# Four row buffers in the scoring stages, and 32 x 32 turns on VectorE in the first layer's chunk softmax, in a graph-attention kernel

## The chip, the cores and the metric

One core of a Trainium2 chip. The metric is the device time of one launch in microseconds (us); the kernel before took 2799.43 us (median of 3 runs, 2797.33 to 2800.22). A change of about 0.2% (5.6 us) is what a measurement of this kernel can tell from none.

## What is computed

Three graph attentions over 3125 nodes with 256 features and 50000 edges sorted by destination, with residual sums and two layer norms. The first attention has 8 heads, the second one, the third 4 (with a vector for each of 64 edge types). Cut to the first:

```python
feat = (h @ fc_w.T).reshape(n, heads, out_feats)
el = jnp.sum(feat * attn_l, axis=-1); er = jnp.sum(feat * attn_r, axis=-1)
e = jax.nn.leaky_relu(el[src] + er[dst], 0.2)
m = jax.ops.segment_max(e, dst, num_segments=n)
ex = jnp.exp(e - m[dst])
ssum = jax.ops.segment_sum(ex, dst, num_segments=n)
rst = jax.ops.segment_sum(feat[src] * (ex / ssum[dst])[..., None], dst, num_segments=n)
```

## The kernel before

**Tiles and stages.** The edges are cut into 416 items of 128 edges, one edge in each partition, none of which crosses a block of 128 destinations. Eight items are a group (52 groups), 32 items a turn or chunk (13). The program is a row of stages, and at each stage's start every engine but GpSimd (POOL) waits for the others: items, node1, score1, sum1, node2, score2, soft2, sum2, node3, score3, soft3, sum3, final. The engines meet through semaphores that are written out by hand; each runs its own instruction list in order.

**Gathers (lines 700 to 752).** POOL issues one indirect DMA for each item and each table (line 735): 416 of layer 1's features (`tab_feat1`, 256 features and 8 `el` terms), 416 of layer 2's, 416 rows of K and 416 of V. The rows land in a ring of 8 slots of 8 items (4 slots for K). A slot is gathered anew when its reader has released it: in sum1 by `slot_used` on the multiply of line 1961, in sum2 by `sum_mm` from the matmuls of line 929. POOL runs ahead of the stages as far as the ring lets it.

**Scores.** For each group, SyncE broadcasts the block-local destinations of its 1024 edges to all partitions, 128 KB (lines 574 and 547; in score2 and score3 a second DMA brings the low source numbers or the types). VectorE compares them with its partition number and so has one-hot rows (line 1761 in score1, 1531 in score2; in score3 ScalarE does it, line 1275). TensorE multiplies them with the tables of `er` and `el` (line 971; lines 849 and 852), VectorE reads the products (1767; 1568 and 1577, between them the one-hot 1554 of the next group) and then makes the one-hots of the group after the next. There are two buffers of broadcast rows (`bcast`), of one-hots (`onehot_t`) and of products, used in turn (s % 2). SyncE issues a group's rows when `onehot_made[s % 2]` shows that the one-hots of two groups before are made. Once in two groups TensorE loads 16 block numbers into registers (`blocks`, line 822), since the matmuls address their table by them.

**sum1 (lines 983 to 1062 and 1836 to 2001).** The first layer's softmax is done chunk by chunk beside its weighted sums. For a chunk `c + 1`, VectorE adds `el` and `er` when the last of its four slots has landed (`make_logits`); TensorE turns the logits so that two items of a head lie in each of 128 lanes (`transposed`); VectorE scans them for running maxima in both directions (`lane_tops`); TensorE turns the two columns of lane ends into one row of partition 0 (`lane_ends`, lines 995 and 996), where VectorE scans over the lanes (`stitch`); TensorE turns the two rows of carries back into columns (`carries`, 1001 and 1002), and VectorE scans again with them and computes the exponentials (`numerators`). TensorE turns the result back (`shares`, line 1009) and makes the factors (`factors`, 1014) by which the open bank of sums is rescaled (`rescale`). Between these steps stand the four groups of the chunk in work: `build(c, half, g)` makes the one-hot rows (1954) and weighted rows (1961, 1965) of group g in two buffers used in turn, and TensorE adds them up in PSUM (line 1024, 16 instructions for a group). VectorE's order in a period is

```python
rescale(c); make_logits(c + 1); build(1); lane_tops(c + 1); build(2)
stitch(c + 1); build(3); numerators(c + 1); factor_terms(c + 1); build(c + 1, 0)
```

Of the kernel before, what the change touches and what calls it, by code (L numbers as in the profile page):

```python
# [29 lines left out]
P = 128  # L30
# [67 lines left out]
def graph_layers(nc, a, out):  # L98
    ctx = ExitStack()
    with ctx:  # L100
# [88 lines left out]
        def views(*sizes):  # L189
            got, at = [], 0  # L190
            for n in sizes:
# [36 lines left out]
        bcast = v[0][:, 0:GROUP * P].bitcast(U8).rearrange("p (s a e) -> p s a e", s=2, a=2)  # L228
        bcast_words = v[0][:, 0:GROUP * P].bitcast(I16).rearrange("p (s a e) -> p s a e", s=2, a=2)
# [17 lines left out]
        gate0, gate1, from_left, from_right, before_row, after_row = (v[7][0:1, k * P:(k + 1) * P] for k in range(6))  # L247
        tail_row = v[7][0:1, 6 * P:6 * P + H1 * (LANES + 1)].rearrange("p (h j) -> p h j", h=H1)
        crossing, factor_rhs, factor, carry_cols = v[8], v[9], v[10], v[11]
# [71 lines left out]
        bcast_in = [sem(f"item_rows_broadcast{s}") for s in range(2)]  # L321
# [13 lines left out]
        logits_made, logits_t, ends_made, ends_t, stitched, carried, numer_made, shares_in, factor_in, factor_made = (  # L335
            sem("chunk_" + k) for k in ("logits_made", "logits_transposed", "lane_ends_made", "lane_ends_in_rows",
                                        "carries_made", "carries_in_columns", "numerators_made", "shares_in_psum",
# [79 lines left out]
        TR_BANK, W_BANK, ROW_BANK = 0, 1, 2  # L417

        def broadcasts(layer):

            return 16 * HALF + 32 * HALF * (layer - 1) if layer else 0

        @block.sync
        def _(sp):
# [108 lines left out]
            def score_rows(layer, name, first):  # L533
# [35 lines left out]
            with nc.sync.Fori(0, TURNS) as u:  # L569
                for s in range(SLOTS):  # L570
# [3 lines left out]
                    sp.dma_start(bcast_words[:, s % 2, 1], row.partition_broadcast(P)).then_inc(bcast_in[s % 2], 16)  # L574
# [62 lines left out]
        def _(pool):  # L637
# [13 lines left out]
            for credit in slot_used + onehot_made + score_read + sort_row_used:  # L651
# [102 lines left out]
        def _(pe):  # L754
# [76 lines left out]
            def gat_scores(layer, name, heads):  # L831
# [5 lines left out]
                with nc.tensor.Fori(0, TURNS) as u:  # L837
                    for s in range(SLOTS):
# [3 lines left out]
                        pe.wait_ge(onehot_made[s % 2], nth(u, s) + (layer * HALF + 2))  # L842
# [17 lines left out]
            def pair_scores(layer, name):  # L860
# [3 lines left out]
                with nc.tensor.Fori(0, TURNS) as u:  # L864
                    for s in range(SLOTS):
# [3 lines left out]
                        pe.wait_ge(onehot_made[s % 2], nth(u, s) + (layer * HALF + 2))  # L869
# [87 lines left out]
            def er_pass(name):  # L957
# [4 lines left out]
                with nc.tensor.Fori(0, TURNS) as u:  # L962
                    for s in range(SLOTS):
# [3 lines left out]
                        pe.wait_ge(onehot_made[s % 2], nth(u, s) + 2)  # L967
# [15 lines left out]
            def chunk_sums(name):  # L983
# [9 lines left out]
                def lane_ends(c):  # L993
                    pe.wait_ge(ends_made, c + 1)
                    nc.tensor.matmul(ps[0:1, ROW_BANK, 0:P], heads_top[:, 0:1], ident[:], start=True, stop=True)
                    nc.tensor.matmul(ps[0:1, ROW_BANK, P:2 * P], tops[:, SPAN - 1:SPAN], ident[:], start=True,
                                     stop=True).then_inc(ends_t, 1)

                def carries(c):
                    pe.wait_ge(stitched, c + 1)  # L1000
                    nc.tensor.matmul(ps[:, ROW_BANK, 2 * P:2 * P + 1], before_row, ones[0:1, 0:1], start=True, stop=True)
                    nc.tensor.matmul(ps[:, ROW_BANK, 2 * P + 1:2 * P + 2], after_row, ones[0:1, 0:1], start=True,
                                     stop=True).then_inc(carried, 1)

                def shares(c):
                    pe.wait_ge(numer_made, c + 1)
                    by_lane = ps[:, W_BANK, 0:SPAN].rearrange("p (j x h) -> p x h j", x=2, h=H1)
# [1218 lines left out]
```

## Time and profile before

| | before |
|---|---|
| median of 3 runs | 2799.43 us |
| the profiled execution's own time | 2800.09 us |
| its span in the trace | 2798.3 us |
| TensorE's mean granted clock | 0.75 of full speed |
| busy: PE, PEld, DVE, ACT, POOL | 61%, 44%, 54%, 15%, 59% |

The span is what the trace covers; 1.8 us lie around it. PE is TensorE's matmuls, PEld its weight loads, DVE is VectorE, ACT ScalarE, POOL GpSimd, SP SyncE. "q" behind an engine's name is its sequencer. A row of a timeline has the start, the duration, the engine, the line of the kernel, the operation, what it writes and reads, and in brackets how long the engine had been idle and what ended that idle time ("issue": nothing that the profile shows). No engine is near 100%, so that a reader has to go by stages. On the time axis the stages lie about so: score1 143 to 265 us, sum1 to 786, node2 to 884, score2 to 1027, soft2 to 1048, sum2 to 1503, node3 to 1627, score3 to 2150, soft3 and sum3 to 2690, final to 2798.

### The profile page before, as it was taken

To read this page: it belongs to the slowest core of one execution; us is meant where nothing else is said; L and a number is where in the kernel's file an instruction comes from. 1 tells how busy PE (TensorE), PEld (TensorE's weight loads), DVE (VectorE), ACT (ScalarE), POOL (GpSimd) and SP (SyncE) were. 2 spreads that over 40 slices of the span, in tenths; PEclk is the share of its full clock that TensorE was granted. 3 is DMA by queue.
4 is the path that set the end of the run, shared out by engine and by line. 5 is a ranking of instruction groups with operands and counts; after the bars stand their busy time and mean duration, and the time that the engine had idled before them with its cause. 6 is when DMAs were issued, how large, how long until landed. Compare 5 with 4: busy or idle time off the path is not lost.

```text
span 2798.3 us, 30721 instructions
## 1 busy us (share of the span) xinstructions
PE 1710.9 (61%) x7623; PEld 1226.0 (44%) x7624; DVE 1518.8 (54%) x2334; ACT 430.0 (15%) x909; POOL 1659.1 (59%) x1791
## 2 busy tenths in 40 slices
PE   3844555555587437655655977777776465565654
PEld 1433434343455436444443445555554344444443
DVE  3245766756745876333334646666766633333348
ACT  0200000000021000000001444444442100000024
POOL 0072777777302816777773057777777777777720
PEclk8855777777788558687776977778878667768679
DMA  0363333333213633333332344444444333333322
GB/s 25 104 154 89 97 105 106 105 106 106 56 54 106 172 93 95 104 104 105 105 104 64 107 122 130 131 130 131 131 130 120 98 105 104 105 105 104 105 64 69
DMA packets 166454, 290.04 MB, mean 104 GB/s; under 512 B 37842, under 2 KB 113035, under 8 KB 166411
## 3 DMA queue, kind: packets, MB, share of 16 engines
q0 software_dynamic: 79872, 219.91, 27.4%
q1 hardware_dynamic: 86539, 69.66, 9.4%
q8 instruction: 14, 0.23, 0.0%
q14 instruction: 29, 0.24, 0.0%
HBM read 272.74 MB, written 16.68 MB: 103 GB/s over the span
## 4 chain that ended last, share of the span: by engine, by line
POOL 46%; issue 22%; DVE 11%; PE 9%; DMA 9%; SPq 1%; POOLq 1%; DVEq 1%; ACT 0%; ACTq 0%
POOL row_space L735 45%; DMA arena<-rows_block_dst 6%; PE ps L1024 2%; DVE arena L1961 2%; PE ps L810 2%; PE ps L1075 2%; DVE arena L1531 1%; DMA row_space<-tab_k,index_slot 1%; DMA row_space<-tab_feat,index_slot 1%; DVE arena L1954 1%; PE ps L1077 1%; DVE arena L1761 1%; POOL index_slot L710 1%; PE ps L802 1%; PE ps L775 1%
## 5 line engine op out<-in xcount | busy, mean ns | idle before, releaser
L735 POOL DMA_INDIRECT row_space<-tab_feat,index_slot x832 | 832.6, 1001 | 368.7 <-issue 235.0
L929 PE MATMUL ps<-row_space,arena 128*128 128x257 f32 (+1 forms) x1664 | 581.8, 526 | 383.0 <-DVE row_space L1722 383.0
L929 PEld LDWEIGHTS ps<-row_space,arena 128*128 128x128 f32 x1664 | 445.5, 274 | 519.2 <-issue 419.4
L1721 DVE TENSOR_TENSOR row_space<-row_space,ps 128x2048 f32<-128x2048 f32 x104 | 237.6, 2285 | 579.6 <-DMA row_space<-tab_v,index_slot 303.4
L735 POOL DMA_INDIRECT row_space<-tab_v,index_slot x416 | 402.8, 968 | 123.8 <-issue 118.8
L735 POOL DMA_INDIRECT row_space<-tab_k,index_slot x416 | 394.0, 947 | 123.8 <-issue 116.4
L1024 PE MATMUL ps<-arena 128*128 128x265 f32 x832 | 253.4, 469 | 102.6 <-DVE arena L1965 53.0
L883 PE MATMUL ps<-row_space,arena 128*128 x832 | 288.9, 508 | 0.0
L710 POOL COPY index_slot<-src_i 128x16 int32 (+1 forms) x104 | 25.3, 243 | 405.1 <-SPq L426 404.8
L1024 PEld LDWEIGHTS ps<-arena 128*128 128x128 f32 x832 | 190.8, 235 | 154.5 <-issue 112.4
L1217 ACT COPY acc<-ps 128x265 f32<-128x265 f32 (+2 forms) x75 | 28.3, 377 | 1420.6 <-PE ps L929 919.4
L883 PEld LDWEIGHTS ps<-row_space,arena 128*128 128x128 f32 x832 | 198.6, 250 | 39.0
L1613 DVE TENSOR_TENSOR arena<-row_space,ps 128x1024 f32<-128x1024 f32 x104 | 126.4, 1215 | 162.7 <-DMA row_space<-tab_k,index_slot 131.2
L877 PE MATMUL ps<-rel_stack,arena 128*128 128x64 bf16 x416 | 88.3, 212 | 125.8 <-DVE arena L1621 111.7
L1715 DVE TENSOR_TENSOR arena<-ps,block_dst 128x1024 f32<-128x1024 f32 x104 | 126.1, 1213 | 14.3 <-ACT ps L1203 14.3
L1621 DVE TENSOR_TENSOR arena<-arena,ps 128x1024 f32<-128x1024 f32 x104 | 127.0, 1221 | 9.7 <-DVE arena L1613 5.4
L877 PEld LDWEIGHTS ps<-rel_stack,arena 128*128 128x128 bf16 x416 | 41.1, 99 | 186.7 <-DVE arena L1621 158.1
L1603 DVE TENSOR_REDUCE scores<-arena 128x2048 f32 (+1 forms) x52 | 118.5, 2280 | 0.0
L1961 DVE TENSOR_TENSOR arena<-row_space,ps 128x2048 f32<-128x2048 f32 x52 | 118.4, 2276 | 0.0
L849 PE MATMUL ps<-el_parts,arena 128*128 128x25 bf16 x1248 | 60.8, 183 | 81.5 <-DVE arena L1531 75.3
L1275 ACT ACTIVATE arena<-arena,minus_type_no 128x1024 bf16<-128x1024 uint8 x52 | 59.7, 1147 | 285.3 <-PE ps L883 277.0
L971 PE MATMUL ps<-er_parts,arena 128*128 x416 | 56.2, 199 | 72.5 <-DVE arena L1761 60.0
(316 smaller groups left out, 2091.6 us busy)
## 6 DMA issues: line engine op xcount, KB each, us to landing
arena<-rows_block_dst SPq DMA_DIRECT2D x156, 128.0 KB
row_space<-tab_feat,index_slot POOLq DMA_INDIRECT x832
arena<-rows_src_low SPq DMA_DIRECT2D x52, 128.0 KB
arena<-rows_type SPq DMA_DIRECT2D x52, 128.0 KB
row_space<-tab_k,index_slot POOLq DMA_INDIRECT x416
row_space<-tab_v,index_slot POOLq DMA_INDIRECT x416
arena<-in_x_t SPq DMA_DIRECT2D x50, 128.0 KB, 2.2
tab_feat<-arena SPq DMA_DIRECT2D x25, 132.0 KB, 1.8
```

The lines of the kernel that those rows point to most:

```text
L735: nc.gpsimd.indirect_dma_start(wide_rows[:, s, g, 0:(D if n else WIDE)], None, table, bass.IndirectOffsetOnAxis(ap=index_slot[:, s, g:g + ...
L849: nc.tensor.matmul(ps[:, bank, at:at + w], onehot_t[:, s % 2, 0, e], el_parts[:, k, 0:w], start=k == 0, stop=k == 2)
L877: nc.tensor.matmul(relation, type_onehot[:, s % 2, e], rel_stack[:, 0, :], start=True, stop=False)
L883: last = nc.tensor.matmul(ps[:, bank, at:at + D], query_onehot[:, s % 2, g * P:(g + 1) * P], query[:, bass.ds(bs[g], 1), :].rearrange("p a ...
L929: last = nc.tensor.matmul(ps[:, SUM_BANKS:2 * SUM_BANKS][:, bank, 0:width].rearrange("p a d -> p (a d)"), onehots_of[:, s, g, :], wide_row ...
L1024: last = nc.tensor.matmul(ps[:, SUM_BANKS:2 * SUM_BANKS][:, bass.ds(banks[s % 2 * GROUP + g], 1), 0:AW].rearrange("p a d -> p (a d)"), one ...
L1603: vec.tensor_reduce(by_item(H3)[:, bass.ds(u * STEP + s * GROUP, GROUP), :], pair_product[:, s % 2].rearrange("p i (h d) -> p i h d", h=H3 ...
L1613: then(vec.tensor_tensor(pair_product[:, z, items, :].rearrange("p i (h d) -> p i h d", h=H3), rows[:, s, items, :].rearrange("p i (h d) - ...
L1621: vec.tensor_tensor(pair_product[:, z, items, :], pair_product[:, z, items, :], ps[:, 2 * half:2 * half + 2, :].rearrange("p q (i d) -> p ...
L1715: vec.tensor_tensor(onehots_of[:, s], ps[:, SHARE_BANK:SHARE_BANK + 1, IOTA_AT:IOTA_AT + P].broadcast_to([P, GROUP, P]), block_dst[:, bass ...
L1721: vec.tensor_tensor(row, row, share.unsqueeze(3).broadcast_to([P, GROUP, heads, D // heads]), ALU.mult)
L1961: vec.tensor_tensor(weighted[:, z, :, 0:D].rearrange("p i (h d) -> p i h d", h=H1), wide_rows[:, half * SLOTS + g, :, 0:D].rearrange("p i ...
```

## The change

First, `bcast` has four buffers of rows, one for each group of a turn, with four semaphores; the one-hots still have two. SyncE gets its credit for them once more (two for each of the two semaphores), and the waits of TensorE on `onehot_made` are one higher, so that only SyncE runs two groups further ahead. This is in score1, score2 and score3.

Second, in sum1 the lane ends and the carries are turned by VectorE, in 32 x 32 blocks: eight `vec.transpose` for the two columns of ends and eight for the two rows of carries; the four small matmuls and their three waits are gone. The softmax of chunk `c + 1` is no longer spread between the groups: `lane_tops`, `stitch`, `numerators` and `factor_terms` run in one piece behind `build(2)` and ahead of `build(3)`. TensorE turns the shares and makes the factors ahead of the fourth group. The shares have two banks of PSUM, used in turn; the factors move to the bank of the turned logits. TensorE's loop holds two chunks instead of one.

```diff
-        bcast = v[0][:, 0:GROUP * P].bitcast(U8).rearrange("p (s a e) -> p s a e", s=2, a=2)
+        bcast = v[0].bitcast(U8).rearrange("p (s a e) -> p s a e", s=SLOTS, a=2)
...
-            for credit in slot_used + onehot_made + score_read + sort_row_used:
+            for credit in slot_used + onehot_made + onehot_made + score_read + sort_row_used:
...
-                            sp.dma_start(bcast_words[:, s % 2, k], row.partition_broadcast(P)).then_inc(bcast_in[s % 2], 16)
+                            sp.dma_start(bcast_words[:, s, k], row.partition_broadcast(P)).then_inc(bcast_in[s], 16)
...
-                        pe.wait_ge(onehot_made[s % 2], nth(u, s) + (layer * HALF + 2))
+                        pe.wait_ge(onehot_made[s % 2], nth(u, s) + (layer * HALF + 3))
...
-                    if not last:
-                        lane_ends(c + 1)
                     banks, cleared = sum_banks(c, 2)
                     group_sums(c, 2, banks, cleared)
                     if not last:
-                        carries(c + 1)
+                        shares(c + 1, 1 - half)
+                        factors(c + 1)
                     group_sums(c, 3, banks, cleared)
-                    if not last:
-                        shares(c + 1)
-                        factors(c + 1)
...
-                dve.wait_ge(bcast_in[z], nth(u, s) * 32 + (32 + broadcasts(layer)))
-                vec.tensor_scalar(onehot_t[:, z], bcast[:, z], part_no[:], None,
+                dve.wait_ge(bcast_in[s], u * 32 + (32 + broadcasts(layer)))
+                vec.tensor_scalar(onehot_t[:, z], bcast[:, s], part_no[:], None,
                                   ALU.is_equal).then_inc(onehot_made[z], 1)
...
+                    all_but(0)
+                    for k, edge in enumerate((heads_top[:, 0:32], tops[:, SPAN - 32:SPAN][:, ::-1])):
+                        for q in range(0, P, 32):
+                            last = vec.transpose(end_rows[:, k * P + q:k * P + q + 32], edge[q:q + 32])
+                    then(last)
...
+                    for k in range(2):
+                        for q in range(0, P, 32):
+                            turned = vec.transpose(carry_blocks[q:q + 32, k * 32:(k + 1) * 32],
+                                                   row_block[:, (4 + k) * P + q:(4 + k) * P + q + 32])
+                    then(turned)
...
-                    each(vec.tensor_copy(carry_cols[:, 0:2], ps[:, ROW_BANK, 2 * P:2 * P + 2]))
...
                     build(c, half, 1)
-                    if not last:
-                        lane_tops(c + 1)
                     build(c, half, 2)
                     if not last:
-                        stitch(c + 1)
+                        soft_chunk(c + 1)
+                        factor_terms(c + 1)
                     build(c, half, 3)
                     if not last:
-                        numerators(c + 1)
-                        factor_terms(c + 1)
                         build(c + 1, 1 - half, 0)
```

## Rows read from the trace of the kernel before

**Rows 1.** The page's chain that ended last: shares of the span.
```profile
POOL row_space L735 45%; DMA arena<-rows_block_dst 6%; PE ps L1024 2%; DVE arena L1961 2%; PE ps L810 2%; PE ps L1075 2%; DVE arena L1531 1%; DMA row_space<-tab_k,index_slot 1%; DMA row_space<-tab_feat,index_slot 1%; DVE arena L1954 1%; PE ps L1077 1%; DVE arena L1761 1%; POOL index_slot L710 1%; PE ps L802 1%; PE ps L775 1%
```

**Rows 2.** Stretch of score2: length, busy us (count) of each engine, PE clock, DMA share, GB/s.
```profile
884.00:1027.00 143.00, 62.77 (x1665) 58.64 (x1666) 116.32 (x216) 0.00 (x0) 91.41 (x68) 0.50 0.55 154
```

**Rows 3.** Line 735's own view: ns min/median/max, releasers of its engine's idle time.
```profile
L735 POOL DMA_INDIRECT row_space<-tab_k,index_slot x416: 942/946/975, 1627.2 to 2148.4; - x139
...
  PE ps L929: 63.3, 1
  DVE arena L1961: 61.3, 18
```

**Rows 4.** Timeline of POOL, sum1: start us, us, instruction, idle before and releaser.
```profile
284.56 1.06 POOL L735 DMA_INDIRECT row_space<-tab_feat,index_slot  x1 [56.09 <-DVE arena L1961]
...
520.73 0.97 POOL L735 DMA_INDIRECT row_space<-tab_feat,index_slot  x1 [0.16 <-POOL index_slot L710]
...
734.22 0.95 POOL L735 DMA_INDIRECT row_space<-tab_feat,index_slot  x1 [0.30 <-issue]
```

**Rows 5.** Line 1531's own view, score2's one-hots on VectorE.
```profile
L1531 DVE TENSOR_SCALAR arena<-arena,part_no x52: 1277/1286/1521, 887.4 to 1022.5; 128x2048 bf16<-128x2048 uint8 x52
```

**Rows 6.** Timeline of score2, all engines.
```profile
1002.87 1.28 DVE L1531 TENSOR_SCALAR arena<-arena,part_no 128x2048 bf16<-128x2048 uint8 x1 [0.79 <-DMA arena<-rows_block_dst]
...
1004.74 0.39 SPq L547 DMA_DIRECT2D arena<-rows_block_dst  x1
...
1004.98 1.28 DVE L1531 TENSOR_SCALAR arena<-arena,part_no 128x2048 bf16<-128x2048 uint8 x1
```

**Rows 7.** The chain in order of time: start us, us, what.
```profile
951.04 3.87 DMA arena<-rows_block_dst
...
1004.74 3.01 DMA arena<-rows_block_dst
```

**Rows 8.** Timeline of TensorE, score2.
```profile
1002.02 0.23 PE L849 MATMUL ps<-el_parts,arena 128*128 128x25 bf16 x3 [1.72 <-DVE arena L1531]
...
1004.21 0.26 PE L849 MATMUL ps<-el_parts,arena 128*128 128x25 bf16 x3 [0.99 <-DVE arena L1531]
...
1007.43 0.26 PE L849 MATMUL ps<-el_parts,arena 128*128 128x25 bf16 x3 [2.03 <-issue]
```

**Rows 9.** Line 822's own view, PE's register load.
```profile
L822 PEldq TENSOR_LOAD <-block_i x78: 1102/1105/1298, 138.5 to 2131.2; - x78
```

**Rows 10.** Timeline of TensorE, score1, with gathers running and after they stopped.
```profile
190.63 2.18 PE L971 MATMUL ps<-er_parts,arena 128*128 x16 [2.17 <-DVE arena L1761]
194.58 2.19 PE L971 MATMUL ps<-er_parts,arena 128*128 x16 [1.76 <-DVE arena L1761]
...
240.41 2.21 PE L971 MATMUL ps<-er_parts,arena 128*128 x16 [2.12 <-issue]
```

**Rows 11.** Timeline of VectorE, start of sum1.
```profile
270.07 0.28 DVE L1876 COPY arena<-ps 1x128 f32<-1x128 f32 x1 [1.10 <-PE ps L996]
...
272.49 0.16 DVE L1904 COPY arena<-ps 128x2 f32<-128x2 f32 x1 [0.71 <-PE ps L1002]
```

**Rows 12.** Timeline of VectorE, one period of sum1.
```profile
491.52 0.59 DVE L1859 TENSOR_TENSOR arena<-row_space,scores 128x256 f32<-128x256 f32 x1 [11.81 <-DMA row_space<-tab_feat,index_slot]
...
495.96 0.67 DVE L1867 TENSOR_TENSOR_SCAN arena<-arena,ps 128x256 f32<-128x256 bf16 x1
...
502.14 0.28 DVE L1876 COPY arena<-ps 1x128 f32<-1x128 f32 x1 [1.34 <-PE ps L996]
...
503.66 0.16 DVE L1890 TENSOR_TENSOR arena<-arena 1x8 f32<-1x8 f32 x1
...
515.85 1.22 DVE L1954 TENSOR_TENSOR arena<-ps,block_dst 128x1024 f32<-128x1024 f32 x1
517.00 2.28 DVE L1961 TENSOR_TENSOR arena<-row_space,ps 128x2048 f32<-128x2048 f32 x1
```

**Rows 13.** Groups by line: busy us, mean ns, idle before.
```profile
L1928 DVE TENSOR_SCALAR arena<-iota_free,arena 128x128 f32<-128x128 f32 x12 | 3.4, 280 | 0.0
```

More of the change, by code:

```diff
@@ L320, in graph_layers @@
         slot_used = [sem(f"rows_used{s}") for s in range(2 * SLOTS)]
-        bcast_in = [sem(f"item_rows_broadcast{s}") for s in range(2)]
+        bcast_in = [sem(f"item_rows_broadcast{s}") for s in range(SLOTS)]
         onehot_made = [sem(f"onehot_made{s}") for s in range(2)]
@@ L416, in graph_layers @@
         HALF = GROUPS // 2
-        TR_BANK, W_BANK, ROW_BANK = 0, 1, 2
+        TR_BANK, W_BANKS, FACTOR_AT = 0, (1, 2), 2 * P
         def broadcasts(layer):
-            return 16 * HALF + 32 * HALF * (layer - 1) if layer else 0
+            return 16 * TURNS + 32 * TURNS * (layer - 1) if layer else 0
         @block.sync
@@ L991, in transposed, with shares @@
                     last.then_inc(logits_t, 1)
[L993 to L1005, printed above, removed]
+                def shares(c, half):
                     pe.wait_ge(numer_made, c + 1)
-                    by_lane = ps[:, W_BANK, 0:SPAN].rearrange("p (j x h) -> p x h j", x=2, h=H1)
+                    by_lane = ps[:, W_BANKS[half], 0:SPAN].rearrange("p (j x h) -> p x h j", x=2, h=H1)
                     for x in range(2):
@@ L1029, in group_sums, with period @@
                             last.then_inc(sum_mm, 1)
-                def period(c, first, last):
+                def period(c, half, first, last):
                     banks, cleared = sum_banks(c, 0)
@@ L1044, in period @@
                     if not last:
-                        carries(c + 1)
+                        shares(c + 1, 1 - half)
+                        factors(c + 1)
                     group_sums(c, 3, banks, cleared)
-                    if not last:
-                        shares(c + 1)
-                        factors(c + 1)
                 transposed(0)
-                lane_ends(0)
-                carries(0)
-                shares(0)
-                period(0, True, False)
-                with nc.tensor.Fori(0, CHUNKS - 2) as u:
-                    period(u + 1, False, False)
-                period(CHUNKS - 1, False, True)
+                shares(0, 0)
+                period(0, 0, True, False)
+                with nc.tensor.Fori(0, (CHUNKS - 3) // 2) as u:
+                    period(u * 2 + 1, 1, False, False)
+                    period(u * 2 + 2, 0, False, False)
+                period(CHUNKS - 2, 1, False, False)
+                period(CHUNKS - 1, 0, False, True)
                 pe.wait_ge(sum_mm, QUADS + TICKS + CREDIT)
@@ L1868, in lane_tops @@
                     all_but(0)
-                    vec.tensor_tensor_scan(heads_top[:, ::-1], gap_now[:, 1:SPAN + 1][:, ::-1], tops[:, ::-1], -BIG,
-                                           ALU.add, ALU.max).then_inc(ends_made, 1)
+                    then(vec.tensor_tensor_scan(heads_top[:, ::-1], gap_now[:, 1:SPAN + 1][:, ::-1], tops[:, ::-1], -BIG,
+                                                ALU.add, ALU.max))
+                    all_but(0)
[3 more added lines that the diff above has]
+                    then(last)
                 def stitch(c):
-                    head, tail = (by_head(ps[0:1, ROW_BANK, k * P:(k + 1) * P]) for k in range(2))
-                    dve.wait_ge(ends_t, c + 1)
+                    head, tail = (by_head(end_rows[0:1, k * P:(k + 1) * P]) for k in range(2))
+                    all_but(0)
                     then(vec.tensor_copy(tail_row[:, :, 1:LANES + 1], tail))
@@ L1885, in stitch @@
                     all_but(1)
-                    vec.tensor_tensor_scan(before_row, gate0, from_left, -BIG, ALU.add, ALU.max).then_inc(stitched, 1)
-                    dve.wait_ge(stitched, c + 1)
+                    then(vec.tensor_tensor_scan(before_row, gate0, from_left, -BIG, ALU.add, ALU.max))
+                    all_but(0)
                     last = by_head(from_left)[:, :, 0:1]
@@ L1933, in rescale @@
                     dve.wait_ge(factor_made, c)
-                    then(vec.tensor_scalar(factor, ps[:, ROW_BANK, 2 * P + 8:2 * P + 8 + H1],
+                    then(vec.tensor_scalar(factor, ps[:, TR_BANK, FACTOR_AT:FACTOR_AT + H1],
                                            not_cross[:, bass.ds(c, 1)], None, ALU.add))
@@ L1993, in chunk_sums @@
                 with vec.Fori(0, (CHUNKS - 3) // 2) as u:
-                    step.enter(u, 2 * 32)
+                    step.enter(u, 2 * 35)
                     period(u * 2 + 1, 1, u, False, False)
```

40 lines of the change are left out of this document (21 added, 19 removed).

## The prediction

> **What bounds the kernel now.** I read the page's chain first [rows 1]: POOL's gather issue, line 735, holds 45% of the span, the landing of the broadcast rows 6%. A share of a chain says who was late last, not what would be late next, so I went through the stages.
>
> In score3, POOL issues 416 gathers from 1627.2 to 2148.4 us, 1.256 us from one to the next, at a median of 0.946 us each and a gap of 0.30 [rows 3]. So it never waits there, and it goes straight on to the V gathers of soft3 and sum3: up to 2690 us nothing but POOL sets the time. In sum1, POOL goes from 284.56 to 734.22, that is 351 steps of 1.281 us [rows 4], and VectorE stands idle 11.81 us in each period for the last rows of the next chunk [rows 12]: POOL again. But POOL has two long waits. One of 56.09 us ends at 284.56, with the multiply of sum1's first group [rows 4]; one of 63.3 us ends with the first sums of sum2 [rows 3]. In both it has filled the eight slots during the score stage and waits for the sum stage to begin. So score1 and score2 are on the path in full: a microsecond saved there moves all of what follows, up to the length of these waits.
>
> Score2. The one-hots of 52 groups start from 887.4 to 1022.5 [rows 5], which is 2.65 us a group. The one-hot at 1002.87 came 0.79 us late, held by the rows' DMA; the next had no such wait, and from one to the other are 2.11 us [rows 6]: this is VectorE's own work for a group. The broadcast loop: one-hots of 1.28 us, second issue 1004.74, which is 0.59 us after they end at 1004.15 [rows 6], landing after 3.01 to 3.87 us [rows 7]: 4.88 to 5.74 us for two groups, 2.44 to 2.87 each. That is the observed pace. TensorE's matmuls of a group take 1.19 us (the next group found it idle for 2.03 us up to 1007.43, so it had ended at 1005.40, having begun at 1004.21), and ahead of every other group there is an idle time of 2.03 or 1.72 us [rows 8]. In it lies the load of block numbers, 1.105 us [rows 9], which comes only when the matmuls before it are out.
>
> Score1. The chain names the broadcasts here too, but TensorE's rows speak against them. Its idle time ahead of a pair of groups is 2.17 and 1.76 us by turns while the gathers run, and 2.12 us later, where the profile names no releaser but "issue" [rows 10]. The pace, 3.95 us from 190.63 to 194.58, doesn't improve when the DMA queues are quiet. A pair costs 2.19 us of matmuls and the register load around it: (2 x 2.19 + 2.15 + 1.76) / 2 = 4.15 us. The broadcasts land just as the load ends; they aren't what binds.
>
> **The change part by part.**
>
> (a) Four row buffers in score2. The broadcast loop may now last four groups. At 2.2 us a group that is 8.8 us, less 1.87 us for one-hots and issue leaves 6.9 us for the landing, against 3.87 now. The DMA engines are busy at a share of 0.55 in this stage [rows 2], which a pace 1.2 times as quick raises to 0.66. So the wait of VectorE goes. What is late next is a loop through both engines: one-hots of an odd group end; 0.06 to TensorE (1004.15 to 1004.21 [rows 6, 8]); 1.19 of matmuls; 2.03 with the register load; 1.19 for the even group's matmuls; about as short a way back; then two whole groups of VectorE's work, 2 x 2.11, up to the end of the one-hots four groups on, 0.09 past the start of what follows. In all 8.8 us for four groups, 2.20 a group. The floors from rows are 2.11 (VectorE alone) and (4 x 1.19 + 2.03 + 1.72) / 4 = 2.13 (TensorE alone). 51 x (2.65 - 2.20) = 23 us. I take 22, since four groups' rows are now issued ahead of the first one-hots and share the queues. Bounds: 27.5 us at VectorE's floor; 12 us if the landing rises so that 2.42 is the pace, about the best that the broadcast loop shows now.
>
> (b) Four row buffers in score1. The register load stays. Gain 0.4 us, for the few pairs where rows came after the load. Bounds 0 and 22 us; the upper one is all idle time beyond the load's 1.105 us, (1.96 - 1.105) x 26.
>
> (c) Four row buffers in score3. POOL issues without a break [rows 3], so 0. What hides it is 521 us of gather issue; without that, it would be worth ScalarE's few waits.
>
> (d) The sixteen transposes. No row shows one. A small VectorE instruction that must wait for the one before starts 0.2 us later (line 1890 takes 0.16 us [rows 12]), and 128 elements a partition take 0.28 us [rows 13]; a block turn handles 32. Between 0.10 and 0.28 I take 0.19, near the small ones: 16 x 0.19 = 3.0 us a chunk. Here the Trainium skill bears on it: its page "VectorE: DVE Perf Modes" (section "Two Vector instructions with no wait between them") says that an instruction whose operand starts in another group of 32 partitions than the last one's starts only when all earlier ones are finished, and this is so for each of these blocks. By the formula of its section on the TRN2 errata, (32 + 151) / 0.96, that is an estimate of 0.19 us each and the same 3.0 us; if they overlapped, it would be nearer 0.10 and 1.6 us. No row here shows it.
> What goes: waits of 1.10 us for the ends and 0.71 us for the carries plus the copy out of PSUM, 0.2 us with its wait [rows 11]. At the head of sum1, ahead of the first released slot, all lies on POOL's wait: 3.0 - 2.0 = 1.0 us lost (bounds -0.4 and +2.5).
>
> (e) The softmax in one run, steady state. VectorE's period has 11.81 us of slack [rows 12], so 1 us more of work costs nothing there. But the order changes when slots are released. `build(2)` follows `build(1)` and is earlier than before. `build(3)` is later. From the landing at 491.52: `build(1)` ends at 495.96; `build(2)` takes another 3.43 (as from 515.85 to 519.28), 499.4; `lane_tops` 1.4 (before, it and `build(2)` filled 495.96 to 502.14 less the wait of 1.34), 500.8; ends 1.5; stitch 1.6 (502.14 to 503.66 and a step more) and 0.2; carries 1.5; numerators and factors 8.1 (before, 503.66 plus 0.4 for two steps and 3.43 for `build(3)` is 507.5, and from there to 515.85 less the copy that goes); so `build(3)` begins about 513.9 and its multiply, 1.15 + 2.28, ends at 517.4 to 517.6. Now POOL comes to this slot at 520.73 [rows 4]. So 3 us of cover remain and the cost is 0. Without the cover it would be one for one, in 11 periods. `rescale` then waits for the sums of the fourth group, which now start at the end of `build(3)`; 4 to 5.5 us later it is about 524, well ahead of the next landing at about 532. Behind the waiting `rescale` stand the make_logits, which wait for the rows anyway. The gathers stay at 1.281 us.
>
> (f) The last chunk, where no gather hides VectorE. The wait for the lane ends goes (1.34 us or more), the transposes come, and `rescale` waits 2 us for sums that had long been done. I take +0.5 us, bounds -2 and +4.
>
> The sum against the profiled execution: 2800.1 - 22 - 0.4 + 0 + 1.0 + 0 + 0.5 = 2779.2 us. The median of the runs is 0.7 lower, so 2778.5 us.
>
> **The rivals.**
>
> A. The landing of rows grows with eight DMAs in the queue beside the gathers. For it: the gathers ran when it was 3.87 us, and it was 3.01 without them [rows 7]. Against it: the loop allows 6.9 us. It would leave 12 us or less of (a): 2788 us.
>
> B. Score1's load is no floor, and the four buffers speed it up too. For it: the profile names VectorE's one-hots as releaser in the first 85 us. Against it: the same idle times later without that [rows 10]. With most of the 22 us bound: 2762 us.
>
> C. The slot of the fourth group is released too late, and POOL, which has no slack of its own, waits in every period of sum1. It decides from 16 transposes of together 3.0 + 3.0 us, 0.38 us each. Each microsecond beyond costs 11, and the head and the tail pay from the first one. At 0.45 us a transpose, (7.2 - 6.0) x 11 + 2 x 4.2 = 21.6 us, the gain is gone; at 0.5 us it is (8 - 6) x 11 + 2 x 5 = 32 us, and the kernel takes 2810 us. For it: no row bounds a block turn with its own latency, and sixteen come in a row. Against it: every VectorE instruction of 128 elements or fewer takes under 0.3 us.
>
> D. The four buffers don't run ahead, because something else holds SyncE (the credits, the issue time of 0.39 us each). Then only (d) to (f) remain: 2801 us. Against it: two issues a group are 0.8 of 2.2 us.
>
> **How the numbers follow.** Forecast as summed, between 2774 and 2783: 0.74. A 0.10, B 0.06, C 0.04, D 0.06. The likeliest is 2778.5. The range goes from 2772 (VectorE's floor in score2) to 2790 (A, with the bounds of (d) and (f)); B, C and D lie outside. A measurement tells 0.2%, 5.6 us, from no change. Faster: forecast, A and B, 0.90. The same: D, 0.06. Slower: C, 0.04.
>
> **What would show it.** In the profile after: score2's one-hots from first to last in about 112 us instead of 135, with no wait for rows; TensorE's register load ahead of each even group as now; POOL's wait ahead of sum2 about 41 us instead of 63.3; TensorE's pairs in score1 still 4.15 us apart; transposes of about 0.2 us; POOL without a wait in sum1's periods and still 1.28 us a gather; score3 unchanged. The prediction is wrong if the pace in score2 stays over 2.4 us, if POOL waits for line 1961 in mid sum1, or if the gathers slow down beside the transposes.

## The result, and the profile after

The changed kernel takes 2782.17 us (median of 4 runs, 2781.04 to 2782.65), the kernel before beside it 2798.38 us (2796.92 to 2800.22): a ratio of 0.9941, 95% interval 0.9925 to 0.9957, or 16.2 us less. The forecast was 2778.5, within 2772 to 2790. The profiled execution took 2782.65 us and spans 2780.5 us, 17.8 less than before's span. Runs e5 to e12 below were made while every kernel, the one before too, took some 18% longer (3318 us for it) for a cause that no row names, e5 to e8 on the same chip as e1 to e4 and e9 to e12 on another, so their whole times are set only against the kernel before beside them.

Line numbers of after: the gather is 737 (735 before), score2's one-hots 1517 (1531), score1's 1747 (1761), `er`'s matmul 973 (971), the register load 824 (822), the multiply 1956 (1961), `rescale` 1936 (1941), the new transposes 1860 and 1885.

Score2's one-hots and the gathers, in the views of their own lines (as [rows 5], [rows 3]):

```profile
L1517 DVE TENSOR_SCALAR arena<-arena,part_no x52: 1272/1277/1526, 890.8 to 1006.2; 128x2048 bf16<-128x2048 uint8 x52
its engine sat idle before it (us, times) until:
  DMA arena<-rows_block_dst: 3.4, 2
```

```profile
L737 POOL DMA_INDIRECT row_space<-tab_k,index_slot x416: 942/946/973, 1609.8 to 2131.0; - x139
...
  DVE arena L1956: 68.0, 22
  PE ps L931: 31.3, 3
```

Score2 is 115.4 us from first to last one-hot, against 135.1. Of its 44 waits for broadcast rows two are left; before, line 1531's view had

```profile
its engine sat idle before it (us, times) until:
  DMA arena<-rows_block_dst: 25.1, 44
```

Score3 is untouched: 521.2 us both times.

TensorE in score1, as [rows 10], and POOL at the head of sum1, at the fourth group's slot and at the end, as [rows 4]:

```profile
192.85 2.20 PE L973 MATMUL ps<-er_parts,arena 128*128 x16 [2.19 <-issue]
196.79 2.19 PE L973 MATMUL ps<-er_parts,arena 128*128 x16 [1.74 <-issue]
201.13 2.21 PE L973 MATMUL ps<-er_parts,arena 128*128 x16 [2.15 <-issue]
...
242.62 2.22 PE L973 MATMUL ps<-er_parts,arena 128*128 x16 [2.14 <-issue]
```

```profile
288.96 1.05 POOL L737 DMA_INDIRECT row_space<-tab_feat,index_slot  x1 [61.63 <-DVE arena L1956]
...
523.34 0.97 POOL L737 DMA_INDIRECT row_space<-tab_feat,index_slot  x1 [0.16 <-issue]
...
735.86 0.95 POOL L737 DMA_INDIRECT row_space<-tab_feat,index_slot  x1 [0.30 <-issue]
...
1041.06 0.94 POOL L737 DMA_INDIRECT row_space<-tab_feat,index_slot  x1 [30.97 <-PE ps L931]
```

The idle times ahead of TensorE's pairs of groups are those of before (2.19 and 1.74 us, against 2.17 and 1.76); only the name of the releaser has changed from the one-hots to "issue". VectorE's timeline, first the start of sum1 and then one period, as [rows 11, 12]:

```profile
270.58 0.69 DVE L1853 TENSOR_TENSOR_SCAN arena<-arena,ps 128x256 f32<-128x256 bf16 x1 [0.86 <-PE ps L992]
271.31 0.69 DVE L1855 TENSOR_TENSOR_SCAN arena<-arena 128x256 f32<-128x256 bf16 x1
272.03 1.70 DVE L1860 STREAM_TRANSPOSE arena<-arena 32x32 f32<-32x32 f32 x8
...
275.14 1.70 DVE L1885 STREAM_TRANSPOSE arena<-arena 32x32 f32<-32x32 f32 x8
...
486.82 0.43 DVE L1936 TENSOR_TENSOR ps<-ps,arena 128x256 f32 x1 [3.19 <-PE ps L1014]
...
494.38 0.59 DVE L1845 TENSOR_TENSOR arena<-row_space,scores 128x256 f32<-128x256 f32 x1 [6.67 <-DMA row_space<-tab_feat,index_slot]
...
518.35 2.28 DVE L1956 TENSOR_TENSOR arena<-row_space,ps 128x2048 f32<-128x2048 f32 x1
...
527.64 0.43 DVE L1936 TENSOR_TENSOR ps<-ps,arena 128x256 f32 x1 [3.29 <-PE ps L1014]
```

A transpose takes 0.21 us from start to start (eight in 1.70). The fourth group's multiply (the row at 518.35) ends at 520.63, POOL comes to that slot at 523.34: 2.7 us of cover. The 11.81 us of idle VectorE have become 6.67, and 3.2 in front of `rescale`.

With marks at the same events, the 17.8 us less of span add up so (us; plus is time lost):

| stretch | before | after | change |
|---|---|---|---|
| up to the first one-hot of score1 | 150.62 | 153.13 | +2.51 |
| score1, to the first memset of sum1 | 114.03 | 113.74 | -0.29 |
| head of sum1, to POOL's release | 19.91 | 22.09 | +2.18 |
| POOL's first to last gather of sum1 | 449.66 | 446.90 | -2.76 |
| from there to the last sums' start | 43.61 | 45.56 | +1.95 |
| node2 | 109.54 | 109.33 | -0.21 |
| score2, first to last one-hot | 135.14 | 115.41 | -19.73 |
| to the first sums of sum2 | 28.80 | 28.75 | -0.05 |
| the rest | 1746.99 | 1745.59 | -1.40 |

### The profile page after: what moved, and what is told of

Same layout as the page of the kernel before. It is cut to its first block, busy times and chain, and to the rows that moved or that the text cites. A ratio compares the mean times of both kernels' runs of the same rounds, so it can differ in the third digit from the quotient of the medians.

```text
span 2780.5 us, 30703 instructions
## 1 busy us (share of the span) xinstructions
PE 1701.3 (61%) x7519; PEld 1225.7 (44%) x7520; DVE 1555.6 (56%) x2529; ACT 429.7 (15%) x909; POOL 1668.2 (60%) x1791
## 4 chain that ended last, share of the span: by engine, by line
POOL 40%; issue 25%; DVE 18%; PE 10%; DMA 3%; DVEq 1%; POOLq 1%; SPq 1%; ACT 0%; ACTq 0%
POOL row_space L737 40%; DVE arena L1956 3%; PE ps L812 2%; PE ps L1061 2%; DMA row_space<-tab_feat,index_slot 1%; DVE arena L1517 1%; PE ps L973 1%; DVE arena L1916 1%; PE ps L1014 1%; PE ps L931 1%; DMA row_space<-tab_k,index_slot 1%; PE ps L1063 1%; DVE arena L1949 1%; DVE arena L1860 1%; DVE arena L1747 1%
## 5 line engine op out<-in xcount | busy, mean ns | idle before, releaser
L737 POOL DMA_INDIRECT row_space<-tab_feat,index_slot x832 | 843.3, 1014 | 339.8 <-issue 233.3
```

The costliest lines, as they stand in the source:

```text
L737: nc.gpsimd.indirect_dma_start(wide_rows[:, s, g, 0:(D if n else WIDE)], None, table, bass.IndirectOffsetOnAxis(ap=index_slot[:, s, g:g + ...
```

## The experiments

e1 to e4 share runs of the kernel before of 2805.9 us, e5 to e8 of 3318.9, e9 to e12 of 3317.8. In e5 to e12 the traces have idle stretches that the profile puts to "issue"; what is read from their rows is read inside one stage.

**e1, the four buffers alone.** The kernel before, with the change's buffers and credits and nothing of the softmax. The edits here and below are cut to their main lines.

```diff
-            bcast_in = [sem(f"item_rows_broadcast{s}") for s in range(2)]
+            bcast_in = [sem(f"item_rows_broadcast{s}") for s in range(SLOTS)]
-                        pe.wait_ge(onehot_made[s % 2], nth(u, s) + (layer * HALF + 2))
+                        pe.wait_ge(onehot_made[s % 2], nth(u, s) + (layer * HALF + 3))
```

> The kernel before with the four row buffers alone; the first layer's softmax stays as it was. My theory, from the two traces: of the 17 us gained, all comes from score2, and the softmax part costs about 1.2 us in sum (0.9 for a larger memset, 1.4 at the head and 2.0 at the tail of sum1, less 2.8 of quicker gathers). So 1 us under the changed kernel, 17.5 us under the kernel before, a ratio of 0.9937. Rival: the softmax part costs the missing 4 us or more: 21 us under the kernel before. Second rival, that the softmax part is what brings the gain: no faster than before.

Measured: 2778.9 us, ratio 0.9908 (0.9893 to 0.9923), which is 25.8 us less by the ratio and 27.0 by the medians. My theory (17.5 us less) was missed; the rival that the softmax costs 4 us or more said 21. Score2's one-hots:

```profile
L1531 DVE TENSOR_SCALAR arena<-arena,part_no x52: 1268/1277/1424, 887.0 to 1000.9; 128x2048 bf16<-128x2048 uint8 x52
its engine sat idle before it (us, times) until:
  DMA arena<-rows_block_dst: 2.6, 1
```

**e2, the softmax alone.** The changed kernel, with SyncE held two groups ahead.

```diff
-                        sp.wait_ge(onehot_made[s % 2], nth(u, s) + (layer * HALF + 1))
+                        sp.wait_ge(onehot_made[s % 2], nth(u, s) + (layer * HALF + 2))
...
-                    sp.wait_ge(onehot_made[s % 2], nth(u, s) + 1)
+                    sp.wait_ge(onehot_made[s % 2], nth(u, s) + 2)
```

> The changed kernel, in which SyncE waits one count longer in all three score stages, so that only two groups' rows are ahead as before. It leaves the softmax part of the change alone. My theory: 1.2 us over the kernel before, ratio 1.0004. Rival that it costs the missing 4 us: ratio 1.0015 to 1.002. Rival that it is what gains: 0.996 or less.

Measured: 2809.27 us, ratio 1.0013 (1.0004 to 1.0022), so 3.4 us more than before: my theory was 1.2 us, the rival 4. Score2's waits for rows are back (28.7 us, 44 times). By the ratios e1 is worth -25.8 us and e2 +3.6, together -22.2; e3, which has both but for score1's buffers, -21.6.

Why e1 gained more than the whole change did can be read from the traces of e1 and e2, which were run together. With two groups ahead (e2) score2's one-hots span 139.3 us, with four (e1) 113.9; score1's `er` matmuls take 113.9 and 110.8 us. So here the buffers were worth 25.4 us in score2 and 3.1 in score1, where they were worth 19.7 and 0.3 between the two kernels' own traces (135.1 and 111.4 before). Four ahead takes nearly the same time in both measurements, two ahead does not (135.1 and 139.3 us), so that the gain is larger where two ahead waits longer for its rows. Why it waited longer is not known.

**e3, score1 alone back to two ahead.** Of e2's edit the second line, the one of score1's loop, only.

> The changed kernel with SyncE only two groups ahead in score1, four in score2 and score3. My theory: TensorE's pair of groups stays 4.15 us in score1, since the register load binds it, and the first broadcast lands 1.5 us earlier because two instead of four share the queues: 1 us under the changed kernel. Rival, that score1 gained from the four buffers and the load is no floor: 5 us or more over the changed kernel.

Measured: 2785.63 us, ratio 0.9923 (0.9909 to 0.9937), which overlaps the changed kernel's 0.9941 (0.9925 to 0.9957). TensorE's first to last `er` matmul takes 112.3 us, against 111.1 with four ahead in the changed kernel (110.8 in e1, on e3's chip) and 111.4 in the kernel before. The one-hots wait for rows 33 times, 49.4 us together: a wait with many entries that is worth 1.2 to 1.5 us, because most of the time would pass anyway.

**e4, one register load for four groups.** e1 with 32 block numbers in one load a turn, where two loads of 16 were.

```diff
-                pe.load(regs[0:2 * GROUP], block_i[0:1, bass.ds(u * STEP + s * GROUP, 2 * GROUP)])
+                pe.load(regs, block_i[0:1, bass.ds(u * STEP, STEP)])
```

> e1 with the block numbers of a whole turn, 32, loaded into TensorE's registers at once, instead of 16 twice. My theory: the load binds score1, so one of the two idle times of 1.75 and 2.15 us in each of 13 turns goes, less what a longer load costs: 13 x (1.2 to 1.75) = 16 to 23 us. In score2 the loop through both engines shortens towards VectorE's floor of 2.11 us a group, from 2.25: 4 to 6 us more. Together 20 to 28 us under e1. Rival, that the load lies beside other work: within 3 us of e1.

Measured: 2796.98 us, ratio 0.9969 (0.9958 to 0.9979), 18 us slower than e1, where I had expected 20 to 28 us faster: a miss. The views of the load's line, here and in e5, to be set against the 1102/1105/1298 ns of [rows 9]:

```profile
L822 PEldq TENSOR_LOAD <-block_i x39: 2128/2138/2333, 141.2 to 2110.6; - x39
```

```profile
L822 PEldq TENSOR_LOAD <-block_i x156: 587/592/1387, 138.8 to 2540.5; - x156
```

A load costs by the number: 592, 1105 and 2138 ns for 8, 16 and 32, some 64 ns each and 75 ns besides. One load for two saves nothing in score1 (111 us as before). In score2 the load in one piece does harm: TensorE idles some 3.5 us ahead of a turn (3.6 in score1), more than two buffers of one-hots cover, and the pace falls to (1022.0 - 890.8) / 51 = 2.57 us a group, 131.2 us where e1 has 113.9.

**e5, eight numbers a load.** e1 with a load for each group.

> e1 with eight block numbers loaded into TensorE's registers ahead of every group instead of 16 ahead of every other. e4 showed that the load costs by the number (2.14 us for 32, 1.11 for 16). Theory, that score2's pace is the loop through TensorE's load and VectorE's two buffers: a group's TensorE time becomes even, 1.19 + 0.95 = 2.14 to 2.2 us, next to VectorE's 2.11, so the pace goes from 2.23 to 2.14 to 2.2 us, 2 to 4 us under e1; score1 unchanged at 4.15 us a pair. Rival, a load has a fixed cost of some 0.4 us beside the numbers: 20 us over e1, most of it in score1.

Measured: 3261.1 us, ratio 0.9854 (0.9786 to 0.9922). Where score1 runs undisturbed, four groups take 8.9 us, against 8.28 with loads of 16. In score2's quiet stretch the one-hots follow at 2.10, 2.10, 2.09 and 2.64 us, as with loads of 16, and not evenly at 2.14 to 2.2 as I had expected. No gain.

**e6 and e11, no load.** e1 without the load in the score stages, run twice. One load ahead of each stage remains, and all groups use its 16 block numbers.

```diff
-                pe.load(regs[0:2 * GROUP], block_i[0:1, bass.ds(u * STEP + s * GROUP, 2 * GROUP)])
```

> e1 without the loads of block numbers in the three score stages: 16 numbers are loaded once ahead of each stage and used for all groups, so the products of er and of the queries are taken from wrong blocks. Theory, the load binds score1 and takes part in score2's loop: score1's pair goes from 4.15 us to 2.3 to 2.7 us, 38 to 48 us less, and score2's pace to VectorE's 2.11 us, 6 us less; score3 unchanged, since the gathers bind it. In all 44 to 54 us under e1. Rival, the broadcast rows bind score1 as the chain says: at most 10 us under e1, with VectorE waiting for rows.

> Four buffers alone, and the loads of block numbers into TensorE's registers in the three score stages are left out (every group uses the blocks of the first load, so its scores are wrong): a measure of what the load costs. In undisturbed stretches of its first run the groups of score1 followed at 1.46 us instead of 2.07 and those of score2 at 2.10 instead of 2.24. Theory (the load binds score1 before as after, so four buffers can't help it): score1's one-hots to the memset of sum1 fall from 113.5 to about 82 us, score2's from 113.9 to 107, 35 to 45 us faster than four buffers alone. Rival (the distance of the buffers or the VectorE binds score1): under 15 us faster.

Measured: 3223.05 us, ratio 0.9731 (0.9649 to 0.9813), and 3221.4 us, ratio 0.9688 (0.9650 to 0.9726). TensorE in score1 in e11:

```profile
252.71 2.22 PE L973 MATMUL ps<-er_parts,arena 128*128 x16 [0.98 <-DVE arena L1763]
255.39 2.19 PE L973 MATMUL ps<-er_parts,arena 128*128 x16 [0.46 <-DVE arena L1763]
258.52 2.23 PE L973 MATMUL ps<-er_parts,arena 128*128 x16 [0.94 <-DVE arena L1763]
```

Two pairs take 5.81 us, against 8.28 with the load (192.85 to 201.13 above). So the load holds score1: 0.62 us a group, some 32 us in all. With it gone, TensorE waits for the one-hots. In a quiet part of score2 the one-hots follow at 2.09 to 2.11 us without exception, where with the load (e8) every fourth step is about 0.5 us longer, as in the changed kernel below. There the load costs 0.14 us a group. I expected 44 to 54 us (e6) and 35 to 45 us (e11) under the four buffers. By the ratios e6 is 41 us under e8, near the 32 and 7 us of the rows, but each of the two intervals is some 54 us wide, so the whole times settle nothing. No clean run says what the kernel without its load would take.

**e8, three ahead.** e1 with SyncE three groups ahead instead of four.

```diff
-                        sp.wait_ge(onehot_made[s % 2], nth(u, s) + (layer * HALF + 1))
+                        sp.wait_ge(onehot_made[(s + 1) % 2], nth(u, s) + (layer * HALF + 1 + s % 2))
```

> e1 with SyncE three groups ahead instead of four in all score stages. Theory: the broadcast loop of 4.9 to 5.9 us over three groups is 1.6 to 2.0 us, still under the 2.23 us that the engines' loop takes: within 2 us of e1. Rival, the landing grows with the rows in flight and four are just enough: 5 us or more over e1.

Measured: 3285.3 us, ratio 0.9856 (0.9773 to 0.9939), not to be told from e5; e1 itself was not run beside it, so whether it is within 2 us of e1 isn't shown. Its quiet stretches have the paces of four ahead (2.10, 2.10, 2.10, 2.65 in score2, 2.07 in score1).

**e7, e9, e10, e12, the price of the transposes.** The changed kernel with each transpose made three times (e7, e10) or twice (e9), the further results read by nobody, and the changed kernel itself (e12).

```diff
+                            for r in range(2):
+                                vec.transpose(exp_in[32 * r:32 * r + 32, k * P + q:k * P + q + 32], edge[q:q + 32])
                         last = vec.transpose(end_rows[:, k * P + q:k * P + q + 32], edge[q:q + 32])
```

> The changed kernel with each block turn done three times, the extra ones into space that is free then: 32 more of 0.20 us, 6.4 us a chunk. Theory (the slot of the fourth group is released 2.6 to 2.8 us ahead of POOL's need, beyond which each microsecond costs one in 11 periods): (6.4 - 2.7) x 11 = 41 us, and 6.4 us each at the head and at the tail of sum1, so 50 to 56 us over the changed kernel, with POOL waiting for the multiply once a chunk. Rival, that there is no such cover or that the turns slow the gathers: 80 us or more. Rival, that the slack of VectorE (6.7 us a period) is what counts: 13 us.

> The changed kernel with each of its sixteen transposes a chunk issued twice (the copy's result is read by nobody): a transpose costs 0.41 us instead of 0.21. It is the price at which the prediction let the fourth group's slot begin to be released too late (0.38 us a transpose, 3.0 us of cover; in the changed kernel's own trace the cover is 2.6 us). Theory: 3.3 us a chunk more on VectorE, of which 2.6 are hidden, 0.7 us or more over each of some 12 chunks, and 3.3 us each in full at the head and in the last chunk: 10 to 18 us slower than the changed kernel, and POOL's pace from the first to the last gather of sum1 rises from 446.9 to about 455 us. Rival (the 11.8 us for which VectorE waited for rows is the slack): 5 to 7 us slower, POOL's pace unchanged.

> The changed kernel with each transpose issued three times, once more, on a chip where the time is not scattered (the first run of it fell on one where all kernels took 18 per cent longer). Theory, cover of 2.6 us: 6.6 less 2.6, or 4.0 us, in each of some 12 chunks, 48 us, and 13 us at head and tail: 50 to 65 us slower than the changed kernel, with POOL waiting for VectorE's multiplies once per chunk. Rival (slack of 11.8 us): 13 us slower and no such waits.

> The changed kernel itself, beside the others, so that the doubled and tripled transposes are read against it on the same chip: 16 to 17 us faster than the kernel before, as in its own measurement.

Measured: e7 3368.9 us (1.0188, 1.0119 to 1.0257), e9 3340.2 (1.0134, 1.0085 to 1.0183), e10 3366.9 (1.0133, 1.0095 to 1.0171), e12 3282.9 (0.9875, 0.9827 to 0.9924). The intervals set e9 and e10 apart from e12, not from each other; their traces do. e12 is some 41 us under the kernel before by its ratio, where the same kernel's own measurement had 16 and I expected 16 to 17: one more reason not to carry whole times over from here. POOL's timelines of e12, e9 and e10 in sum1:

```profile
489.46 0.97 POOL L737 DMA_INDIRECT row_space<-tab_feat,index_slot  x1 [13.32 <-DVE arena L1956]
...
544.52 0.97 POOL L737 DMA_INDIRECT row_space<-tab_feat,index_slot  x1 [14.11 <-DVE arena L1956]
```

```profile
450.37 0.97 POOL L737 DMA_INDIRECT row_space<-tab_feat,index_slot  x1 [19.00 <-DVE arena L1961]
...
510.26 0.97 POOL L737 DMA_INDIRECT row_space<-tab_feat,index_slot  x1 [19.58 <-DVE arena L1961]
```

```profile
457.13 0.97 POOL L737 DMA_INDIRECT row_space<-tab_feat,index_slot  x1 [21.35 <-DVE arena L1961]
...
518.87 0.97 POOL L737 DMA_INDIRECT row_space<-tab_feat,index_slot  x1 [21.50 <-DVE arena L1961]
```

Here even the changed kernel has no cover: POOL waits 13 to 16 us for the multiply once in each chunk. The chunks follow at 55.2 us in e12 (nine from 435.13 to 931.63), 59.4 in e9, 61.7 in e10 and 61.6 in e7. From POOL's release at the head of sum1 to score2's first one-hot are 751, 804, 832 and 832 us. So rival C's mechanism is real: once the fourth group's slot is late, each chunk pays. But it was seen only where idle stretches had used up the cover; in the old order too (e11) POOL waits 6 to 10 us for the multiply there.

But the dose was not what I had put down. In e9 a repeated transpose starts 0.14 us behind the first, and a pair takes 0.31 us instead of 0.21, so that e9 added 1.6 us of work a chunk, not 3.3, and e10 4.9, not 6.6; the periods grew by 4.3 and 6.5. Most of what exceeds is idle time of VectorE at "issue", which grew from 11.5 us a chunk in e12 to 13.8 in e9 and 13.3 in e10. VectorE in e12, amid `stitch`:

```profile
574.21 0.20 DVE L1885 STREAM_TRANSPOSE arena<-arena 32x32 f32<-32x32 f32 x1 [1.23 <-issue]
575.60 0.20 DVE L1885 STREAM_TRANSPOSE arena<-arena 32x32 f32<-32x32 f32 x1 [1.19 <-issue]
577.00 0.20 DVE L1885 STREAM_TRANSPOSE arena<-arena 32x32 f32<-32x32 f32 x1 [1.20 <-issue]
```

These have 1.2 us of idle time in front of each. Line 1885 has 79.6 us of it there, at 67 of its 104 transposes, and 1.2 us in the changed kernel's own trace; line 1860, as many transposes, has 1.7 us in both, so that it isn't the instruction that brings it. With the old order the chunks follow there at 51.6 us (e11). My expectations of e9 (10 to 18 us over the changed kernel) and e10 (50 to 65) were missed: they were 57 and 84 us over e12 by the medians, 86 each by the ratios. For e7 (50 to 56 expected) no changed kernel was run beside it. What happens when the cover of 2.7 us ends was not measured without these idle stretches.

## Why the prediction was right, and where not

**Where the bound lies.** Right. Score2's gain of 19.7 us reached the end of the span: what follows it is no longer than before. POOL's wait ahead of sum2 took it up, though it fell to 30.97 us and not, as I had said, to 41. POOL itself became slower while it filled the slots: 68 gathers and index copies took 91.4 us of busy time before [rows 2], 103.5 after. The rows of after say beside what; they are to be set against the one-hots at 990.49 and 992.59, and the gap behind them, under (a):

```profile
990.09 1.79 POOL L737 DMA_INDIRECT row_space<-tab_feat,index_slot  x1 [0.31 <-issue]
992.19 1.79 POOL L737 DMA_INDIRECT row_space<-tab_feat,index_slot  x1 [0.30 <-issue]
994.29 0.94 POOL L737 DMA_INDIRECT row_space<-tab_feat,index_slot  x1 [0.30 <-issue]
```

While a one-hot of 1.28 us runs on VectorE, a gather's issue is stretched. In score2, 15 of 62 gathers before and 6 of 60 after met a one-hot for less than 0.15 us, and none of these 21 took more than 0.97 us; the others took 1.54 us in the mean before and 1.72 after. With the one-hots closer together more gathers meet one, and for longer. The broadcasts aren't the reason: in score3, where they run too but ScalarE makes the one-hots, none of 416 gathers takes more than 0.98 us [rows 3]. No run took the one-hots away, so this rests on the rows alone. The loss is hidden as long as POOL's wait is there.

**(a), score2.** Mechanism right, size a tenth too large: 19.7 us in after's trace, where 22 was forecast. (Between e2 and e1 it was 25.4, as two ahead was slower there.) From the third one-hot on the pace is 2.245 us, and not 2.20. The loop of four groups, put at 8.8 us, takes 8.98; VectorE's one-hots show it, two steps of the usual 2.10 us around one of 2.67:

```profile
990.49 1.28 DVE L1517 TENSOR_SCALAR arena<-arena,part_no 128x2048 bf16<-128x2048 uint8 x1
...
992.59 1.28 DVE L1517 TENSOR_SCALAR arena<-arena,part_no 128x2048 bf16<-128x2048 uint8 x1
994.32 0.39 DVE L1554 TENSOR_TENSOR arena<-ps,arena 128x224 f32<-128x224 f32 x1 [0.46 <-PE ps L854]
...
995.26 1.27 DVE L1517 TENSOR_SCALAR arena<-arena,part_no 128x2048 bf16<-128x2048 uint8 x1
...
997.35 1.28 DVE L1517 TENSOR_SCALAR arena<-arena,part_no 128x2048 bf16<-128x2048 uint8 x1
```

The extra 0.5 us every fourth group is the wait for TensorE's products, and e11 shows that it goes with the load. The load alone is not all of it: loads come every second group in this kernel and every group in e5, but the long step comes once a turn in both. Once a turn, ahead of the first group, TensorE's idle time is longer, 2.04 us against 1.66 here and 1.43 against 0.91 in e5; what fills it no row names, and it was not tested alone. Rival A would have shown waits for rows; there are two, 3.4 us.

**(b), score1.** Right: 0.3 us (put at 0.4), though e3 and e2 against e1 give 1.5 and 3.1 us. e11 shows the load to be the floor once the rows are there, so B falls. The pair, put at 4.15 us, takes 8.28 / 2 = 4.14.

**(c)** right, 521.2 us both times. **D** falls with e1.

**(d), the head of sum1.** The transposes were sized well: 0.21 us against 0.19. The chain from the first scan to the first multiply grew by 1.38 us (13.91 to 15.29), within the bounds of the 1.0. That a transpose doesn't overlap the one before is seen in e7. At line 1861 each repeat's input or output starts in another group of 32 partitions than the last one's, and three take 0.64 us from start to start; at line 1888 the repeats start in the same groups, and three take 0.39:

```profile
327.06 0.41 DVE L1861 STREAM_TRANSPOSE arena<-arena 32x32 f32<-32x32 f32 x2
327.48 0.20 DVE L1862 STREAM_TRANSPOSE arena<-arena 32x32 f32<-32x32 f32 x1
327.70 0.41 DVE L1861 STREAM_TRANSPOSE arena<-arena 32x32 f32<-32x32 f32 x2
...
333.60 0.28 DVE L1888 STREAM_TRANSPOSE arena<-arena 32x32 f32<-32x32 f32 x2
333.82 0.16 DVE L1890 STREAM_TRANSPOSE arena<-arena 32x32 f32<-32x32 f32 x1
333.99 0.29 DVE L1888 STREAM_TRANSPOSE arena<-arena 32x32 f32<-32x32 f32 x2
```

So the Trainium skill's rule holds here as far as the rows go ("VectorE: DVE Perf Modes", section "Two Vector instructions with no wait between them"): a transpose whose input or output starts in another group of 32 partitions starts only when the one before has ended. It also tells why e9 added so little, as its repeats start in the groups of the one before and follow after 0.14 us; I had cited the rule and then put a repeat at the full 0.21.

What I forgot is a step of the diff: the memset ahead of it now clears 32 x 904 instead of a row of 136 elements, 0.81 us instead of 0.17, and VectorE is on the path there. The rows of before and after:

```profile
264.80 0.17 DVE L1840 MEMSET arena<- 1x136 f32 x1
```

```profile
267.19 0.81 DVE L1826 MEMSET arena<- 32x904 f32 x1 [0.24 <-DVE arena L1825]
```

With its later start that is 0.8 us. So the head cost 2.2 us, not 1.0.

**(e), steady state.** Right. The cover was put at 3 us and is 2.7. The multiply's end was put at 517.4 to 517.6 for a landing at 491.52, or 26 us behind it; it is 26.25. The wait that moved, `rescale` behind the fourth group's sums, stands at 3.2 to 3.3 us in the rows and costs nothing. POOL went a little quicker (446.9 us for its steps, 449.7 before); the kernels of e1 to e4 lie between 447.3 and 449.6 in either order, so I ascribe it to nothing.

**(f), the tail.** Mis-sized: 1.95 us instead of 0.5. There `rescale`'s wait is in the open. It is 3.55 us at 772.95, where I took 2 us, with the sums' matmuls only starting when `build(3)` ends.

```profile
772.95 0.43 DVE L1936 TENSOR_TENSOR ps<-ps,arena 128x256 f32 x1 [3.55 <-PE ps L1014]
```

Head and tail together cost 4.1 us where 1.5 was forecast, and e2, 3.4 us slower by itself, roughly agrees. The forecast's gain in span was 20.9 us, the measured one 17.8: 2.3 less from (a) and 2.6 from head and tail, 2.5 lost ahead of the first one-hot, 0.1 less from (b), and 4.4 found in POOL's pace, node2 and the rest, none of which the change was seen to cause. So the 17.8 us stand close to the forecast partly by luck: without these 4.4 us it would have been 13.4. The 2.5 us before the first one-hot are 1.0 us of later issue and a landing after 8.8 us instead of 7.3; e1 to e4 show later starts than before as well, with two ahead too, and I leave their cause open.

The best kernel of those run is thus e1: it has the buffers' gain and not the softmax's cost (2778.9 us, where e3 took 2785.6 on the same chip; the changed kernel itself was not run beside them).

## What to carry to other kernels

Before a second buffer is added, ask of each stage what remains idle when the wait that the profile names is gone: the same edit was worth 20 us where VectorE waited for rows, and 0.3 us where a register load filled the same idle time. Where work is moved in front of the instruction that frees a buffer, the slack to count is that of the buffer's release, not the engine's idle time (2.7 us here, with 6.67 us of idle VectorE beside it); and count each memset of the diff that lies at the head or tail of a stage. And compare only kernels that were measured together: the same four buffers were worth 20 us in one measurement and 28 in another.

## What the runs showed of the hardware

- TensorE's load of registers from on-chip memory costs by the number: 592 ns for 8, 1105 for 16, 2138 for 32. Grouping loads saves 75 ns each and makes the gaps longer.
- VectorE's 32 x 32 transposes of 4-byte elements take 0.21 us from start to start when each works on another group of 32 partitions, and a repeat on the same ones follows after 0.14 us.
- Eight such transposes take 1.70 us. In e12, while every kernel took 18% longer, 67 of the 104 transposes of one line had some 1.2 us of idle time in front of them and those of another line hardly any, and no row names a cause. One chip took 2806 us for the kernel before beside e1 to e4 and 3319 us for it beside e5 to e8.
- POOL's issue of an indirect gather takes 0.95 us, and 1.79 us where VectorE makes one-hots of 128 x 2048 uint8 elements beside it for most of that time. Over score2 the 68 instructions grew so from 91.4 to 103.5 us of busy time when the one-hots came closer together.
